# An attention kernel with packed score blocks: where SyncE loads and copies the sets of q and k, and when VectorE turns finished values

## What is computed

```python
xn = layernorm(x)                                   # x: 8 x 1024 x 256
q = (xn @ Wq.T).reshape(n, s, 16, 16)               # 16 heads of 16
k = repeat((xn @ Wk.T).reshape(n, s, 8, 16), 2)     # 8 key heads, each for 2 heads
v = repeat((xn @ Wv.T).reshape(n, s, 8, 16), 2)
energy = einsum('nqhd,nkhd->nhqk', q, k) - abs(i - j) * 2.0 ** -(head + 1)
attn = softmax(energy / 4, axis=-1)
out = einsum('nhqk,nkhd->nqhd', attn, v).reshape(n, s, 256) @ Wo.T + bo
x_q = clip(round(xn / x_scale), -128, 127); lin = (x_q @ weight_q.T) * x_scale * weight_scale + bias
return x + out + lin
```

## Time and profile before

| | |
|---|---|
| median of three runs | 1682.9 us |
| the profiled execution | 1682.93 us, span 1681.1 us |
| busy, share of the span | PE 90%, DVE 84%, ACT 71%, POOL 63% |
| granted clock of PE, mean | 0.976 of full speed |
| moved by DMA | 138.27 MB on SP's queue, 31.7% of 16 engines |

### The profile page before, as it was taken

One profiled execution on the slowest core, in us unless ns is written; L12 is line 12 of the kernel. 1 busy time (PEld: TensorE's weight loads), 2 busy tenths in 40 slices (PEclk: granted clock), 3 DMA queues, 4 the chain that ended last, 5 costly groups with the idle time before them and its releaser, 6 DMA issues.

```text
span 1681.1 us, 41787 instructions
## 1 busy us (share of the span) xinstructions
PE 1512.6 (90%) x15948; PEld 572.1 (34%) x15948; DVE 1412.1 (84%) x1729; ACT 1187.3 (71%) x2331; POOL 1058.1 (63%) x1596
## 2 busy tenths in 40 slices
PE   6799899999998899898899998999989899898889
PEld 5233332333332333332333333333333333232223
DVE  5889889898888898798898888889888888797881
ACT  3467777677777676677676776767777777676776
POOL 5467777677778676667676676767677675332222
PEclk8999999999999999999999999999999999999999
DMA  7423223333323333233333233333233332211221
GB/s 170 106 62 86 72 76 85 94 89 93 95 71 93 91 87 92 79 89 84 102 85 89 78 85 90 101 81 98 84 84 84 98 80 67 62 53 51 57 56 58
DMA packets 197288, 140.94 MB, mean 84 GB/s; under 512 B 107040, under 2 KB 165728, under 8 KB 197088
## 3 DMA queue, kind: packets, MB, share of 16 engines
q1 hardware_dynamic: 197088, 138.27, 31.7%
HBM read 81.40 MB, written 35.63 MB: 70 GB/s over the span
## 4 chain that ended last, share of the span: by engine, by line
PE 57%; DVE 26%; issue 11%; SPq 4%; DMA 3%; POOL 0%; ACT 0%; DVEq 0%; POOLq 0%; ACTq 0%
DVE row_max L968 23%; PE ps_ring L1248 18%; PE ps_pv L1324 17%; PE ps_row L1265 12%; PE ps_ring L1360 4%; PE ps_ring L1380 3%; DVE pv_turned L1008 1%; PE ps_ring L1363 1%; SPq L454 1%; DMA k<-k_alibi 1%; SPq L458 1%; PE ps_ring L1374 1%; DMA token_dram<-token 1%; PE ps_row L1352 1%; DVE att_normed L1024 0%
## 5 line engine op out<-in xcount | busy, mean ns | idle before, releaser
L968 DVE TENSOR_REDUCE row_max<-ps_row 128x1 f32<-128x1024 f32 x1024 | 1205.6, 1214 | 192.6 <-PE ps_row L1267 182.3
L1140 ACT ACTIVATE probs<-ps_ring 128x512 f32<-128x512 f32 x2048 | 1087.0, 600 | 358.0 <-PE ps_ring L1248 357.0
L733 POOL TENSOR_TENSOR probs<-probs,near 128x256 f32<-128x256 f32 x512 | 374.2, 731 | 459.8 <-ACT probs L1140 451.0
L1248 PE MATMUL ps_ring<-q,k 122*32 122x512 bf16 x8192 | 645.0, 389 | 6.5 <-DMA q<-neg_max_t 5.7
L1324 PE MATMUL ps_pv<-probs,v_unit 128*32 128x512 f32 x4096 | 543.2, 607 | 0.0
L1265 PE MATMUL ps_row<-k,q 64*128 64x512 bf16 x1000 | 347.5, 389 | 138.6 <-issue 80.7
L1248 PEld LDWEIGHTS ps_ring<-q,k 122*32 122x32 bf16 x8192 | 214.3, 96 | 538.9 <-ACT probs L1140 296.8
L1267 PE MATMUL ps_row<-k_again,q_again 64*128 64x512 bf16 x1000 | 348.2, 390 | 0.0
L1265 PEld LDWEIGHTS ps_row<-k,q 64*128 64x128 bf16 x1000 | 86.4, 93 | 446.2 <-issue 291.4
L1324 PEld LDWEIGHTS ps_pv<-probs,v_unit 128*32 128x32 f32 x4096 | 127.3, 111 | 48.3 <-issue 2.7
L1008 DVE STREAM_TRANSPOSE pv_turned<-ps_pv 128x512 f32<-128x512 f32 x64 | 45.9, 717 | 49.6 <-PE ps_pv L1324 49.6
(11 more groups left out here) (83 smaller groups left out, 962.8 us busy)
## 6 DMA issues: line engine op xcount, KB each, us to landing
parts_dram<-parts SPq DMA_DIRECT2D x59, 288.0 KB, 3.7
q_again<-q SPq DMA_DIRECT2D x63, 256.0 KB, 3.1
token_b<-token_dram SPq DMA_DIRECT2D x53, 256.0 KB, 3.8
q<-parts_dram SPq DMA_DIRECT2D x128, 96.0 KB
k<-parts_dram SPq DMA_DIRECT2D x256, 32.0 KB
q<-parts_dram SPq DMA_DIRECT2D x128, 64.0 KB
att_dram<-att_unit SPq DMA_DIRECT2D x126, 64.0 KB
att_t<-att_dram SPq DMA_DIRECT2D x56, 128.0 KB, 2.9
```

The source lines that it names most:

```text
L733: pool.tensor_tensor(here, here, near[:, u % KV_HEADS, :].rearrange("p (e n) -> p e n", e=GROUP), ALU.mult).then_inc(weighted, 1)
L968: dve.tensor_reduce(row_max[:, par, e, qb:qb + 1], ps_row[qb % 2][:, :], AX_X, ALU.max, negate=True).then_inc(row_max_found, 1)
L1140: act.activation(probs[:, c % PBUFS, e, h * HALF:(h + 1) * HALF], ring_bank(u, c, e, h), ACT.Exp, scale=SCALE).then_inc(ring_freed, 1)
L1248: mm = pe.matmul(to[at, :], weights[:, at], moving, start=start, stop=stop)
```

## The change

The load of set u+3 moves from the end of unit u to its beginning (behind the x loads), and its copy to the upper partitions from the beginning of unit u+1 to the end of unit u. This can't be done where the last tile of the sequence is stored only in unit u: for u+3 = 8, 16, 24, 32, 40, 48 and 56 (`late_set`) the load stays at the end, the copy is issued at the end of unit u+1, and the row blocks of slots 8 to 15 that come before it use the old form (`row_block`): eight matmuls on 32 columns each instead of two, with no copy. The wait for the copy stands at slot 8, for these sets at slot 0 of the unit behind. DVE turns finished values after the reduction of slot 3 instead of slot 2.

```diff
+def last_tile(u):
+    return BLOCKS * (u // KV_HEADS + 1) - 1
+
+def late_set(u):
+    return u >= SETS - 1 and last_tile(u) >= PREP_AHEAD and made_unit(last_tile(u)) == u - SETS + 1
@@ SP
             def unit(u, f):
-                if u > 0 and u + 2 < UNITS:
-                    load_again(u + 2, (u + 2) % SETS)
                 if f["next_x"]:
                     next_x(u + X_AHEAD)
                 if f["xt"]:
                     load_xt(u + 2 + PREP_AHEAD)
+                if f["row_set"] and not late_set(u + 3):
+                    next_set(u + 3)
                 if u % PAIR == 1:
                     store_att(u - 1)
...
                 if f["row_set"]:
-                    tiles = u + PREP_AHEAD if u % PAIR == 1 else max(u - 1 + PREP_AHEAD, PREP_AHEAD)
-                    wait_parts(min(tiles, TILES), 0)
-                    if u > 0:
-                        wait_filled(sp, u - 1, BLOCKS - 1, GROUP - 1, 1)
-                    load_set(u + 3, (u + 3) % SETS)
+                    if late_set(u + 3):
+                        next_set(u + 3)
+                    else:
+                        load_again(u + 3, (u + 3) % SETS)
+                if u + 2 < UNITS and late_set(u + 2):
+                    load_again(u + 2, (u + 2) % SETS)
                 for t in finished(u):
                     store_out(t, t % 2)
+            def next_set(u):
+                wait_parts(last_tile(u) + 1, 0)
+                if u >= SETS:
+                    wait_filled(sp, u - SETS, BLOCKS - 1, GROUP - 1, 1)
+                load_set(u, u % SETS)
@@ DVE
-                        if i == 2 and f["prev"]:
+                        if i == 3 and f["prev"]:
                             turn_pv(u - 1)
@@ PE
-                    if i == 0 and u == 0:
+                    if i == 0:
                         wait_again(u + 1)
...
                         wait_row_set(u + 2, (u + 2) % SETS)
-                        wait_again(u + 2)
-                    half_row_block(u + 2, (u + 2) % SETS, 0, i - BLOCKS)
+                        if not late_set(u + 2):
+                            wait_again(u + 2)
+                    if late_set(u + 2):
+                        row_block(u + 2, (u + 2) % SETS, 0, i - BLOCKS)
+                    else:
+                        half_row_block(u + 2, (u + 2) % SETS, 0, i - BLOCKS)
```

## The result

The changed kernel took 1615.07 us (median of four runs, 1614.26 to 1617.88) against 1683.1; the ratio is 0.9601, 95% interval 0.958 to 0.9622. The forecast was 1617. The profiled execution took 1615.71 us, with a span of 1613.9.

What follows compares the result with a forecast made beforehand. PE bounds odd units; in even ones PE and DVE alternate, DVE slightly longer, with PE also waiting for copies queued on SP. 1682.93 - 100 - 15 + 45 + 4 = 1617 us; range 1582 to 1650.

Steps and rivals of the forecast that it cites:

- The waits at slot 8: PE's 39 waits for a set's copy, midway through a unit, would go: 80.7 us plus 19.6 of clock, together -100.
- the rival of new waits at the unit's start: If `place_max` came late in even units, each would lose about 0.8 us: 25 in all, time 1642; chance 0.19.
- The turn: DVE's turn of finished values one block later: 0.5 us saved in each of 31 even units, -15; bounds +3 and -31.
- The late sets: Seven sets copied late make PE wait at slot 0, 5.1 us six times and 4.0 in unit 7, plus clock: +45.
- the stated upper bound of 58: Upper bound on the seven late copies' cost: landing 1.5 us later behind the first copy, and the full 1.9 of clock.
- The clock's part: Slower PE matmuls behind each of the seven waits for a late copy: 1.6 us for six, 1.3 for unit 7.
- The old row blocks: Eight matmuls instead of two in 56 row blocks: 0.6 us a unit, +4 in all; bounds 0 and 13.
- the 2.6 us worked out from it: Estimate for a copy of q from the skill's fixed cost and bandwidth; the trace's 3.1 us was used instead.

## Why the prediction was right

**The waits at slot 8** (-100): they all went, and SP had no new ones to give. Counted in the trace, even units from 2 to 60 were 62 us above their best, odd ones 42, together 104. In the even units from 2 to 60 `place_max` began 14.05 to 15.8 us in, most often 14.05, where it had been 14.7 to 18.3, and the rival of new waits at the unit's start didn't come true in the changed kernel. It did in the kernel with the load moved alone, where the late copies held SP up.

**The turn** (-15): measured -24.7 by the medians and -21 to -22 by the units in the trace, 20.59 us against 21.27 with the turn taken back and 21.30 before. The mechanism was the one described, the size was too small. The idle time of 0.3 us at slot 12, which I let come as new, had been there before; that at slot 8 is new, 0.29 us. DVE's idle time so fell by 0.43 us a unit, and the other 0.25 is busy time, which I hadn't counted: 19.95 us with the turn taken back, 19.71 here, as instructions that follow each other directly overlap in the trace. DVE's timeline of unit 42 after the change, from the reductions to the next idle time:

```profile
1095.10 4.73 DVE L986 TENSOR_REDUCE row_max<-ps_row 128x1 f32<-128x1024 f32 x4 [0.27 <-PE ps_row L1285]
1099.75 0.70 DVE L1026 STREAM_TRANSPOSE pv_turned<-ps_pv 128x512 f32<-128x512 f32 x1
1100.38 2.31 DVE L986 TENSOR_REDUCE row_max<-ps_row 128x1 f32<-128x1024 f32 x2
1102.62 0.23 DVE L1033 RECIPROCAL rsum<-pv_turned 128x16 f32<-128x16 f32 x1
1102.78 2.28 DVE L986 TENSOR_REDUCE row_max<-ps_row 128x1 f32<-128x1024 f32 x2
1105.35 1.22 DVE L986 TENSOR_REDUCE row_max<-ps_row 128x1 f32<-128x1024 f32 x1 [0.29 <-PE ps_row L1285]
```

There is no idle time from the turn to slot 7; before there were 0.47 and 0.23. The forecast added this term to the first. That was right for the change as a whole, but the two don't add: alone, the turn gives nothing.

**The late sets** (+45): measured 56, the term of the sum that was furthest off in us: 43.6 for the waits, where the forecast has 34.6, and 12 for the clock, where it has 10.9. SP's timeline of the changed kernel around the start of unit 15, at 427.55, and PE's block that waits:

```profile
426.14 1.15 SPq L516 DMA_DIRECT2D att_dram<-att_unit  x2
427.39 0.92 SPq L525 DMA_DIRECT2D att_t<-att_dram  x2
428.41 1.41 SPq L497 DMA_DIRECT2D k_again<-k  x1
429.87 0.58 SPq L499 DMA_DIRECT2D q_again<-q  x1
430.54 0.55 SPq L497 DMA_DIRECT2D k_again<-k  x1
431.14 0.59 SPq L499 DMA_DIRECT2D q_again<-q  x1
```

```profile
427.33 0.82 PE L1266 MATMUL ps_ring<-q,k 122*32 122x512 bf16 x12
434.93 0.60 PE L1283 MATMUL ps_row<-k,q 64*128 64x512 bf16 x1 [6.77 <-DMA q_again<-q]
```

The copy of q goes out 3.6 us into the unit, not 2.5, and lands 3.8 later, not 3.1: PE waits 6.77 instead of 5.1. The store of finished values went out 1.4 us before the unit's end, taken as 1.7. It is the first copy's k that takes SP 1.41 us to issue, where 0.56 was taken, and the landing is longer behind another copy. The longer landing is in all seven units, 3.4 to 4.0 us. The slow issue is in three, units 15, 23 and 31, with 1.4 to 1.9 us; in the other four the same instruction takes 0.52 to 0.54, and PE waits 4.6 to 6.2 us instead of 6.8 to 7.3. The 56 us lie inside the stated upper bound of 58. In unit 7, without the loads for the projection, the wait was 4.6 (forecast 4.0). The clock's part was forecast at 1.6 for a wait, 1.3 in unit 7; it was 1.7 on the average.

**The old row blocks** (+4): 21.06 against 20.59 us in seven units, 3.3. The 0.1 us at each change of shape keeps PE's extra work to about 1 us a unit instead of 1.8, and about half of that shows in the unit's length.

Together: -104 - 22 + 56 + 3 = -67, and the spans differ by 67.2. The mechanisms were right, but that the sum is right within 2 us is luck: one term that was 11 us too small stands against two on the other side that were 4 and 7 too small, and these cancel. The largest miss by its share was the turn's.

Two numbers of the prediction need a word. The rival of new waits lets a set's load take 9 us when DMAs are slow; the longest in the trace of the kernel before took 8.5. And the fit of the Trainium skill ("DMA: Bandwidth & Descriptors", Anatomy of one DMA) is for DMAs that GpSimd issues, while SyncE issues these, so the 2.6 us worked out from it were never a price for this copy; nothing in the sum used them.

Left open: why issuing the same copy at the same place of the queue takes 0.54 us in some units and 1.4 to 1.9 in others; no run varied what was in flight at that moment.

## What to carry to other kernels

Here the wait that no engine explained was a transfer's. Such a wait is worth following back on the issuing queue to the first thing that is late, here a load and not the copy behind it, and that one is to be moved. Gains on the engine that waits can be worth nothing while the wait is tied to a queue: the same edit was worth 0 us before the transfers were moved and 21 to 25 after. And an exceptional case that is put last in a queue pays for everything ahead of it; a few lines further up it cost almost nothing, and that was worth 53 to 56 us, almost as much as the change.

## What was not expected of the hardware

Issuing one and the same DMA on SP, at the same place of the queue, took 0.52 to 0.54 us in four units and 1.4 to 1.9 in three. The same 256 KB copy landed 3.1 us after its issue in the median of the kernel before, 3.4 in that of the changed one, and 3.7 to 4.0 right behind another copy in six units. PE lost 0.1 us at each change between matmuls of 64 by 128 and of 128 by 32. Matmuls for 3.9 us in waits of 4.6 to 7.3 us kept the clock at 2.4 GHz behind two of seven; matmuls for 5.6 us kept it up behind all seven. A low clock behind a wait cost 1.0 to 2.4 us, 1.7 on the average.
